# Attention and gated feed-forward on 8 cores: load order, K and V in halves, and the gates among the Q chunks

## What is computed

```python
q = (x @ Wq + bq)          # 16 heads of 64
k = (x @ Wk + bk)          # 2 heads of 64, each for 8 query heads
v = (x @ Wv + bv)
# query s sees keys s-128 ... s+127, zeros beyond the ends (they count in the softmax)
probs = softmax(q . k_window)
attn = (probs . v_window) @ Wo + bo
x = layernorm(x + attn)
W_real = einsum('abcd,cefg->abefdg', G1_R, G2_R).reshape(512, 512)
W_imag = einsum('abcd,cefg->abefdg', G1_I, G2_I).reshape(512, 512)
out_real = x_real @ W_real.T - x_imag @ W_imag.T + bias_real
out_imag = x_real @ W_imag.T + x_imag @ W_real.T + bias_imag
x = layernorm(x + concat(out_real, out_imag))
```

## Time and profile before

| | us |
|---|---|
| median of 3 runs | 517.76 (517.07 to 518.15) |
| the profiled execution | 517.99 |
| its span, slowest core (3) | 516.5 |
| spans of the other cores | 511.6 to 514.7 |
| PE busy on core 3 | 480.7 (93%) |
| DVE, ACT, POOL busy | 370.5, 284.1, 169.0 |

### The profile page before, as it was taken

The page is one execution under the profiler, slowest core; times in us unless marked ns, Lnnn a source line. Parts: engine busy times, 40 slices in busy tenths (PEclk is TensorE's granted clock), DMA queues, the critical chain, the costliest instruction groups (busy, mean ns, idle before and its releaser), DMA issues.

```text
span 516.5 us, 11293 instructions; the slowest of 8 cores (511.6 to 516.5 us)
## 1 busy us (share of the span) xinstructions
PE 480.7 (93%) x3920; PEld 226.2 (44%) x3920; DVE 370.5 (72%) x611; ACT 284.1 (55%) x332; POOL 169.0 (33%) x118
## 2 busy tenths in 40 slices
PE   1598899999999999999999999999999999998995
PEld 1343444444444444444444444444444444443442
DVE  6112467877776788677777777767786777999986
ACT  1337676465564645556555555555545555677633
POOL 8100225233332323333232333313323332433350
PEclk9999899999999999999999999999999999999998
DMA  6999956455455445535543654465434344375333
GB/s 86 150 172 172 248 107 134 113 142 111 119 141 109 127 119 139 139 88 142 144 108 99 143 142 99 128 144 108 114 108 123 83 122 124 103 136 169 85 82 124
DMA packets 82807, 65.15 MB, mean 126 GB/s; under 512 B 67776, under 2 KB 68288, under 8 KB 82752
## 3 DMA queue, kind: packets, MB, share of 16 engines
q1 hardware_dynamic: 75984, 51.17, 37.5%
q0 software_dynamic: 6768, 13.26, 17.2%
HBM read 44.63 MB, written 16.78 MB: 119 GB/s over the span
## 4 chain that ended last, share of the span: by engine, by line
PE 49%; DVE 28%; issue 16%; DMA 3%; ACT 1%; DVEq 1%; POOL 1%; ACTq 0%; POOLq 0%
PE pW L394 16%; PE pW L445 12%; DVE st L722 8%; DVE xb L717 6%; PE pW L425 6%; DVE xr L717 6%; PE pW L459 6%; PE pS L404 5%; DMA XT<-xt 3%; PE pW L379 3%; DVE attn L707 3%; PE pW L384 1%; DVE EX L694 1%; ACT EX L579 1%; DVE xb L777 1%
## 5 line engine op out<-in xcount | busy, mean ns | idle before, releaser
L579 ACT ACTIVATE EX<-pS,shift 128x2048 bf16<-128x2048 f32 x96 | 188.8, 1967 | 108.9 <-PE pS L404 108.9
L342 POOL TENSOR_TENSOR xb<-x,beta_b 128x1024 f32<-128x1024 bf16 x32 | 68.3, 2133 | 212.2 <-DVE x L771 202.8
L394 PE MATMUL pW<-XT,wq_sb 128*128 128x512 bf16 x512 | 120.2, 380 | 0.0
L459 PE MATMUL pW<-wo_sb,attnT 128*128 128x512 bf16 x496 | 116.3, 380 | 0.0
L350 POOL TENSOR_TENSOR xr<-xr,bo_b 128x1024 f32<-128x1024 f32 x32 | 75.5, 2358 | 96.0 <-DVE EX L694 77.9
L694 DVE TENSOR_TENSOR EX<-EX,mask_s 128x2048 bf16<-128x2048 bf16 x64 | 80.5, 1257 | 21.5 <-ACT EX L579 21.5
L717 DVE TENSOR_TENSOR xb<-pW,xb 128x512 f32<-128x512 f32 x62 | 42.5, 686 | 57.0 <-PE pW L445 57.0
L566 ACT ACTIVATE QT<-pW,bq_sb 128x512 bf16<-128x512 f32 x64 | 44.1, 689 | 64.5 <-PE pW L394 62.9
L459 PEld LDWEIGHTS pW<-wo_sb,attnT 128*128 128x128 bf16 x496 | 45.3, 98 | 59.9 <-issue 12.7
L394 PEld LDWEIGHTS pW<-XT,wq_sb 128*128 128x128 bf16 x512 | 46.3, 98 | 49.5 <-issue 2.7
L425 PEld LDWEIGHTS pW<-VB,EX 128*128 128x128 bf16 x1512 | 50.7, 98 | 31.5 <-issue 30.1
(11 more groups left out here) (65 smaller groups left out, 278.7 us busy)
## 6 DMA issues: line engine op xcount, KB each, us to landing
xr<-x SPq DMA_DIRECT2D x32, 512.0 KB, 3.8
y<-xb SPq DMA_DIRECT2D x31, 512.0 KB, 4.3
XT<-xt POOLq DMA_DIRECT2D x32, 256.0 KB, 3.9
wq_sb<-wq POOLq DMA_DIRECT2D x8, 256.0 KB, 22.2
wo_sb<-wo POOLq DMA_DIRECT2D x4, 512.0 KB, 35.7
bo_b<-bo SPq DMA_DIRECT2D x1, 512.0 KB, 8.7
beta_b<-beta SPq DMA_DIRECT2D x1, 512.0 KB, 7.0
y<-xb SPq DMA_DIRECT2D x2, 256.0 KB, 2.2
```

The lines of the kernel that those rows point to most:

```text
L342: gp.tensor_tensor(xb[:, r1 % 4 * D:(r1 % 4 + 1) * D], x1[:, r1 % 2 * D:(r1 % 2 + 1) * D], beta_b, ALU.add).then_inc(gp_b, 1)
L394: i = pe.matmul(p, wq_sb[:, t * 1024 + c * 128:t * 1024 + (c + 1) * 128], rhs_x(g, c), start=c == 0, stop=c == 7)
L459: i = pe.matmul(ps, attnT[:, p % 2 * D + c * 128:p % 2 * D + (c + 1) * 128], wo_sb[:, half * 4096 + c * 512:half * 4096 + (c + 1) * 512], ...
L579: act.activation(EX[:, e0:e0 + 2048], pS, AF.Exp, bias=shift).then_inc(act_e, 1)
```

## The change

Loads: POOL now loads wk, X tiles 0 and 1, wv, X tiles 2 and 3, the first Q weights, the factors of the gates (`gb`), the other Q weights, and then as before; its memsets of KT go behind all of these loads. SP loads the biases first, and dmask, mask and ident only once X tile 3 has landed. PE: K and V of the first group are computed in two halves, each when its two X tiles have landed. Q chunks 0 to 2 follow, then the imaginary gates (G 4 to 7), then Q chunks 3 to 7. The real gates (G 0 to 3) stand behind the first S of turn 0. DVE makes the two products in the other order, the second into a buffer of its own (`gexp`), and copies all gates out in the place of ACT. In turns 0 to 3, two, three, two and one Q chunks are computed instead of two in each, and the first half of `wo` stands before the last S of a turn instead of behind it.

```diff
 EXPOS = {0: 0, 2: 2048, 1: 4096}
+def q_chunks(s):
+    if s == 1:
+        own = [2, 3, 4]
+    elif s == 2:
+        own = [5, 6]
+    elif s == 3:
+        own = [7]
+    else:
+        own = [s % 4 * 2, s % 4 * 2 + 1]
+    return [((s // 4 + 1) * 8 + n, k % 2) for k, n in enumerate(own)]
...
     gb = sb("gb", 576, BF16)
+    gexp = sb("gexp", 8192, BF16)
...
-    wlist = [(("G", n), (n % 4,)) for n in range(8)] + [(("K", 0), (0,)), (("V", 0), (1,))]
-    wlist += [(("Q", n), ((n + 2) % 4,)) for n in range(8)]
+    head = [("K", 0), ("V", 0), ("Q", 0), ("Q", 1), ("Q", 2)] + [("G", n) for n in range(4, 8)] + [("Q", n) for n in range(3, 8)]
+    wlist = [(u, (n % 4,)) for n, u in enumerate(head)]
     for i in range(NT):
         g, j = i // 4, i % 4
         p, o, r = i - 1, i - 2, i - 4
         S = [(("S", 3 * i + k), (4, 5, 6, 7)) for k in range(3)]
         A = [(("A", 2 * p + k), (2, 3)) for k in range(2)] if p >= 0 else []
-        Q = [(("Q", (g + 1) * 8 + 2 * j + k), (k,)) for k in range(2)]
+        Q = [(("Q", n), (b,)) for n, b in q_chunks(i)]
         V = [(("V", (g + 1) * 4 + j), (2,))]
         K = [(("K", g + 1), (3,))] if j == 0 else []
         if r < 0:
             O = [(("O", 2 * o + k), (k,)) for k in range(2)] if o >= 0 else []
-            wlist += S[:1] + A[:1] + Q[:1] + A[1:] + S[1:2] + Q[1:] + V + S[2:] + K + O
+            G = [(("G", n), (n,)) for n in range(4)] if i == 0 else []
+            wlist += S[:1] + G + A[:1] + Q[:1] + A[1:] + S[1:2] + Q[1:2] + V + O[:1] + S[2:] + K + Q[2:] + O[1:]
         elif i < Q_END:
             F = [(("F", 2 * r + k), (2 + k,)) for k in range(2)]
...
-    empties = {"G": act_w, "Q": act_w, "K": act_w, "V": dve_w, "F": dve_w, "O": dve_w, "A": dve_n, "S": act_e, "T": dve_w}
+    empties = {"G": dve_w, "Q": act_w, "K": act_w, "V": dve_w, "F": dve_w, "O": dve_w, "A": dve_n, "S": act_e, "T": dve_w}
     wpos, wbank, wempty, wfree = {}, {}, {}, {}
...
         def _(sp):
-            sp.dma_start(dmask, dmask_d).then_inc(d_dmask, 16)
-            sp.dma_start(mask, mask_d).then_inc(d_const, 16)
-            sp.dma_start(ident, ident_d).then_inc(d_ident, 16)
             sp.dma_start(bq_sb, bq_d).then_inc(d_const, 16)
             sp.dma_start(bk_sb, bk_d).then_inc(d_const, 16)
             sp.dma_start(bv_b, ap(bv_d, 0, [[0, 128], [1, 128]])).then_inc(d_const, 16)
+            sp.wait_ge(d_xt[3], 16)
+            sp.dma_start(dmask, dmask_d).then_inc(d_dmask, 16)
+            sp.dma_start(mask, mask_d).then_inc(d_mask, 16)
+            sp.dma_start(ident, ident_d).then_inc(d_ident, 16)
             def load_r(t):
                 sp.dma_start(xr[:, t % 4 * D:(t % 4 + 1) * D],
...
         @blk.gpsimd
         def _(gp):
-            gp.dma_start(gb, g_d).then_inc(d_gates, 16)
             def load_x(t):
                 gp.dma_start(XT[:, t % 8 * 1024:(t % 8 + 1) * 1024],
                              xt_d[t * 128:(t + 1) * 128, :]).then_inc(d_xt[t % 8], 16)
             gp.dma_start(wk_sb, wk_d).then_inc(d_wk, 16)
-            for t in range(4):
-                load_x(t)
+            load_x(0)
+            load_x(1)
             gp.dma_start(wv_sb, wv_d).then_inc(d_wv, 16)
+            load_x(2)
+            load_x(3)
             for t in range(8):
                 gp.dma_start(wq_sb[:, t * 1024:(t + 1) * 1024],
                              wq_d[:, t * 1024:(t + 1) * 1024]).then_inc(d_wq[t], 16)
-            gp.memset(KT[:, 0:128], 0.0)
-            gp.memset(KT[:, 17 * 128:19 * 128], 0.0)
-            gp.memset(KT[:, 35 * 128:36 * 128], 0.0).then_inc(gp_i, 1)
+                if t == 0:
+                    gp.dma_start(gb, g_d).then_inc(d_gates, 16)
             for t in range(4, 8):
                 load_x(t)
             for h in range(2):
                 for q in range(2):
                     o = h * 4096 + q * 2048
                     gp.dma_start(wo_sb[:, o:o + 2048], wo_d[:, o:o + 2048]).then_inc(d_wo[h], 16)
+            gp.memset(KT[:, 0:128], 0.0)
+            gp.memset(KT[:, 17 * 128:19 * 128], 0.0)
+            gp.memset(KT[:, 35 * 128:36 * 128], 0.0).then_inc(gp_i, 1)
             for i in range(NT + 3):
...
                     pe.wait_ge(d_gates, 16)
-                    pe.wait_ge(dve_g, m + 1)
+                    pe.wait_ge(dve_g, 2 - m)
                 p = take_w(("G", n))
-                gexp = EX if m == 0 else QT
+                product = gexp if m == 0 else EX
                 for e in range(16):
                     i = pe.matmul(p[:, e * 32:(e + 1) * 32],
-                                  gexp[:, e * 512 + dc * 128:e * 512 + (dc + 1) * 128],
+                                  product[:, e * 512 + dc * 128:e * 512 + (dc + 1) * 128],
                                   gb[:, m * 32:(m + 1) * 32], start=True, stop=True)
                 i.then_inc(pe_w, 1)
...
-                        pe.wait_ge(*emptied(("G", 7)))
+                        pe.wait_ge(*emptied(("G", 3)))
                         pe.wait_ge(dve_g, 6)
...
-            for n in range(8):
-                gates(n)
             pe.wait_ge(d_wk, 16)
-            for t in range(4):
-                pe.wait_ge(d_xt[t], 16)
-            k_proj(0)
-            pe.wait_ge(d_wv, 16)
-            p = take_w(("V", 0))
-            for t in range(4):
-                i = v_tile(p, t * 128, t)
+            pk = take_w(("K", 0))
+            pv = take_w(("V", 0))
+            for h in range(2):
+                for t in range(2 * h, 2 * h + 2):
+                    pe.wait_ge(d_xt[t], 16)
+                for c in range(8):
+                    i = pe.matmul(pk[:, h * 256:(h + 1) * 256], wk_sb[:, c * 128:(c + 1) * 128],
+                                  ap(XT, h * 2048 + c * 128, [[8192, 128], [1024, 2], [1, 128]]),
+                                  start=c == 0, stop=c == 7)
+                if h == 0:
+                    pe.wait_ge(d_wv, 16)
+                else:
+                    i.then_inc(pe_w, 1)
+                for t in range(2 * h, 2 * h + 2):
+                    i = v_tile(pv, t * 128, t)
             i.then_inc(pe_w, 1)
             for n in range(8):
+                if n == 3:
+                    for m in range(4, 8):
+                        gates(m)
                 pe.wait_ge(d_wq[n], 16)
                 q_proj(n)
...
+                if s == 0:
+                    for n in range(4):
+                        gates(n)
                 if p >= 0:
                     av(p, 0)
                 if s < Q_END:
                     for landed, n in new_x:
                         pe.wait_ge(landed, n)
                     t = (g + 1) * 4 + j
-                    q_proj((g + 1) * 8 + 2 * j)
+                    q = [n for n, b in q_chunks(s)]
+                    q_proj(q[0])
                     if p >= 0:
                         av(p, 1)
                     if r < 0:
                         scores(s, 1)
-                        q_proj((g + 1) * 8 + 2 * j + 1)
+                        for n in q[1:2]:
+                            q_proj(n)
                         v_tile(take_w(("V", t)), 0, t).then_inc(pe_w, 1)
+                        if o >= 0:
+                            wo(o, 0)
                         scores(s, 2)
                         if j == 0:
                             k_proj(g + 1)
+                        for n in q[2:]:
+                            q_proj(n)
                         if o >= 0:
-                            wo(o, 0)
                             wo(o, 1)
                     else:
-                        q_proj((g + 1) * 8 + 2 * j + 1)
+                        q_proj(q[1])
                         scores(s, 1)
                         ffn(r, 0)
                         ffn(r, 1)
...
-            def gate_out(n):
-                m, dc = n // 4, n % 4
-                act.wait_ge(pe_w, wpos[("G", n)] + 1)
-                dst = wrt if m == 0 else wit
-                act.activation(ap(dst, dc * 512, [[2048, 128], [16, 32], [1, 16]]),
-                               ap(pW, wbank[("G", n)] * 512, [[2048, 128], [1, 32], [32, 16]]),
-                               AF.Copy).then_inc(act_w, 1)
-            for n in range(8):
-                gate_out(n)
-            act.wait_ge(d_const, 4 * 16)
+            act.wait_ge(d_const, 3 * 16)
             k_out(0)
             for n in range(8):
                 q_out(n)
...
-                    q_out((g + 1) * 8 + 2 * j)
+                    q = [n for n, b in q_chunks(s)]
+                    q_out(q[0])
                     if r < 0:
                         ex(s, 1)
-                        q_out((g + 1) * 8 + 2 * j + 1)
+                        for n in q[1:2]:
+                            q_out(n)
                         ex(s, 2)
                     else:
-                        q_out((g + 1) * 8 + 2 * j + 1)
+                        q_out(q[1])
                         ex(s, 1)
                         ex(s, 2)
                         n_ln += 1
```

(34 more changed lines are left out.)

## The result

| | before | after |
|---|---|---|
| median | 517.95 (517.07 to 519.09, 4 runs) | 522.18 (521.64 to 522.33, 4 runs) |
| ratio | | 1.0079 (95% interval 1.0057 to 1.010) |
| profiled execution, its slowest span | 517.99, 516.5 | 522.24, 520.3 |

The change makes the kernel 4.2 us slower; the forecast was 2.4 us faster. Spans and clocks of the changed kernel, to be held against the earlier trace rows: now even the fastest core needs 516.3 us.

The account below looks back on a forecast made before the run. TensorE was taken as the bound, only the first 80 us open to change. First scores at 39.3, plus 474.1 after them and 0.7 for turns, gave a 514.1 span; with 1.5 outside, 515.6, rounded to 515.5 us; range 512.6 to 518.2.

Parts of the forecast that it names:

- Bound: Whole kernel: TensorE is busy for 480.7 of 516.5 us, so the change can only act on the first 80 us.
- term 1: Start: with K and V in halves, Q chunk 2 ends at L + 8.2 at the earliest, perhaps held by its weights.
- L: Start: the landing of X tile 3, forecast at 17.8 us on the slowest core.
- slow phase: Start, 8 to 14 us: core 3 moves 79 GB/s against core 0's 178; forecast to be shortened, not removed.
- Rival B: Start: slow phase goes as small loads leave the first tiles; L 15.1, time 512.9; 0.21 with the end of another rival.
- Term 3: Start, dmask load: takes d as 4.5 us, from 2.2 to 8.7, so the imaginary gates start at L + 10.0.
- d: Start: dmask's time from issue, once X tile 3 has landed, to landing; taken as 4.5 us.
- rival C: Start: dmask late, gain gone from d = 6.9; at 8.7 PE waits 6 us, clock falls, 521.4 us; chance 0.15.
- Term 2: Start: product begins at L + d + 0.2, takes 4.42 us; after V's copy (0.69) gates start at L + d + 5.5.
- Terms 4 and 5: Start: gates 1.87, five Q chunks 8.65, last copy and first scores 1.0, scores at L + d + 17.0; copies moved to DVE cost nothing.
- Turns: Turns 0 to 3: +1.4, 0, +0.5 and -1.2 us, sum +0.7; from turn 4 on the same.
- The clock's fall in turn 2 avoided: Turn 2, core 3: less idle before it keeps the clock from falling to 1.2 GHz, worth 1.4 us.

Follow-up runs that it names:

- f3: Changed kernel with ident (32 KB) issued ahead of dmask behind X tile 3; no median of its own, ident took 7.1 to 7.5 us to land.
- g3: Changed kernel with the imaginary gates behind Q chunk 7 and VectorE's second product ahead of their copies; 522.59 us, ratio 1.01.
- e4: Changed kernel with turns 0 to 3 in the order of before, real gates still behind the first S; 523.72 us in its one execution that counts.
- f2: f1 with 1, 3, 2, 2 Q chunks in turns 0 to 3 and both halves of wo behind the last S; 515.44 us, ratio 0.9948.
- g0: Kernel before with only K and V in two halves and that part's load order; 517.01 us, ratio 1.0.
- e2: Kernel before with VectorE starting the two products only when X tile 3 has landed; 525.8 us.
- f1: Changed kernel with dmask and gb in GpSimd's queue right behind X tile 3, ahead of all Q weights; 517.16 us, ratio 0.9989.
- e1: Changed kernel with dmask loaded first again by SyncE, mask and ident still waiting for X tile 3; 518.07 us, ratio 1.0006.
- h3: g3 with V's copy ahead of the product on VectorE; 520.56 us, ratio 1.0061.
- h4: h3 with 1, 3, 2, 2 Q chunks in turns 0 to 3 and both halves of wo behind the last S; 517.51 us, ratio 1.0007.
- h5: h4 with gb issued behind the fourth load of Q weights instead of the first; 517.59 us, ratio 1.0003.

## Why the prediction was wrong, point by point

The miss is 6.6 us between the sum of 515.6 and the profiled 522.24. On core 1 it splits into 5.1 up to the first S (44.39 against 39.3), 0.45 in turns 0 to 3 (40.77 against 40.3), 0.6 behind them (435.1 against 434.5) and 0.4 outside the span (1.9 against 1.5).

- **Bound, and term 1 (halves)**: right. Q chunk 2 ended 8.5 us behind tile 3, forecast 8.2; 0.4 of it was the wait for its weights that the term named.
- **L**: 17.96 on the slowest core against 17.8, but by another mechanism, so that it came out is luck. The slow phase went wholly, since mask, ident and dmask left the head; the pairs' rate rose by a quarter. Rival B's cause with the forecast's L, since one core of a pair is still late (15.4 and 18.0 on cores 6 and 7).
- **Term 3, the step that failed**: d was 7.2 to 8.5 us, I took 4.5. The range (2.2 to 8.7) held it. I chose by the 2.4 us between bk and bv, a difference of two landings. The landing itself of bv, 9.4 and 13.7 us, was the nearer row; I set it aside because bv stood behind others in its queue. f3 shows that a load at the head of its queue takes 7.3 as well. Cost: d was 3.1 us longer on core 1, the gates started 12.9 us behind L instead of 10.0, and PE's wait was 4.4 us instead of 1.8.
- **The clock**: rival C had it. From 31 to 44 us the granted clock is 0.78, after 4.36 us of idle; 2.0 us on core 1. The central sum had none: this second term, put at nothing, hangs on the first. C's mechanism was right. That its 521.4 is only 0.8 low is in part luck: it was worked out for a d of 8.7; for the measured 7.6 the same working gives 520.3, and the rest is turns 0 to 4 and what follows them. Its chance of 0.15 was too small, since at the moment of the issue eight Q weights and four X tiles were sure to be queued.
- **Term 2**: starts and durations right (product 0.1 us behind dmask, 4.43, V's copy 0.69). That V's copy behind the product also holds a bank of the Q chunks was not seen; in the changed kernel it costs nothing more, in g3 everything.
- **Terms 4 and 5**: right. Tile 7 did not hold PE; DVE's copies held nobody.
- **Turns**: 0: +1.29 (forecast +1.4), 1: 0 (0), 2: +0.37 (+0.5), 3: -0.51 (-1.2). Turn 3 missed the 0.72 us wait for the bank that attention's division (`norm`) empties: with the Q chunk between it and V gone, V comes too early. Turn 4, taken as equal, lost 0.24; undoing the turns' order (e4, f2) removes both. Another 0.4 us behind turn 4 is lost by all kernels built on the changed one; in e4, where I followed it, 0.35 of it arise at one half of av in turn 17, where PE waits 0.27 us for attention's division. Why only there is open.
- **The clock's fall in turn 2 avoided**: right (1.5 us by e4), but core 3 alone does not set the time; a late core of any pair does.
- **Outside the span**: 1.9 us in the changed kernel and all built on it, 1.5 in all built on the kernel before. The cause is open.

## What to carry to other kernels

A small load issued in another queue amid a backlog of big ones took 7 us or more here, whatever its size, and not its own 2: put it into the queue of the big ones, ahead of those that come later, or issue it early enough that its 7 us have cover, and count everything behind its consumer, banks too. Small loads at the head of the start slowed the first big ones, so keep there only what is wanted first. And where all cores load at once, add the rates of the two cores of a pair before you explain the slow one: one core's slow phase may be its neighbour's fast one.

## What the runs showed of the hardware that I had not expected

- 32 KB and 128 KB behind the same backlog: 7.1 to 7.5 and 7.2 to 8.5 us; without it 2.0 to 3.9 for the 128 KB.
- With all six loads of SyncE (293 KB) at the head the pairs move 253 to 287 GB/s from 8 to 14 us (before, g0, e2), with the biases alone (69 KB) 308 to 333 (after, f1).
- The spans of the two cores of a pair deviate in opposite directions: correlations of -0.54 (before, 91 executions), -0.84 (after, 4) and -0.87 (e1, 10).
- In h3, h4 and h5 PE pauses 0.7 to 2.3 us, at 35 to 40 us and at the same matmul on every core, with "issue" as the only reason; behind it the clock falls on seven of the eight cores of h3.
